# Turning the softmax probabilities with a DMA transfer instead of TensorE, in two of three attentions

## The reference, cut to what matters

```python
score = jnp.einsum('bhqd,bhkd->bhqk', q, k) / math.sqrt(DH)     # third: without bias and mask
score = score + position_bias
score = jnp.where(mask, score, -jnp.inf)
probs = jax.nn.softmax(score, axis=-1)
ctx = jnp.einsum('bhqk,bhkd->bhqd', probs, v)
out = ctx.transpose(0, 2, 1, 3).reshape(b, len_q, H * DH) @ Wo
```

## Time and profile before

| | us |
|---|---|
| median of 3 runs | 2335.64 (2335.22 to 2337.76) |
| the profiled execution's own time | 2335.8 |
| its span | 2334.0 |
| TensorE busy | 2173.6 (93%) |
| VectorE busy | 1322.0 (57%) |
| ScalarE busy | 1146.0 (49%) |
| GpSimd busy | 536.4 (23%) |
| TensorE's granted clock, mean | 0.981 of full speed |

### The profile page before, as it was taken

One profiled execution on the slowest core, in us unless ns is written; L12 is line 12 of the kernel. 1 busy time (PEld: TensorE's weight loads), 2 busy tenths in 40 slices (PEclk: granted clock), 3 DMA queues, 4 the chain that ended last, 5 costly groups with the idle time before them and its releaser, 6 DMA issues.

```text
span 2334.0 us, 40760 instructions
## 1 busy us (share of the span) xinstructions
PE 2173.6 (93%) x14284; PEld 1220.1 (52%) x14284; DVE 1322.0 (57%) x2695; ACT 1146.0 (49%) x3004; POOL 536.4 (23%) x936
## 2 busy tenths in 40 slices
PE   4799999999899899999999999998879899999998
PEld 2565555655554445555555555555434455555564
DVE  5566665666740556655656556555642455555654
ACT  4666666666412235554455544533322555666551
POOL 3332332322310312222122221212310222222221
PEclk9999999999989899999999999999979999999999
DMA  3110110110021112111111211101200111111000
GB/s 122 46 47 24 48 43 29 46 35 8 25 108 48 44 70 66 48 66 48 51 62 48 67 48 49 45 12 41 102 25 1 37 37 37 38 46 41 1 33 37
DMA packets 27366, 106.92 MB, mean 46 GB/s; under 512 B 4074, under 2 KB 12522, under 8 KB 17186
## 3 DMA queue, kind: packets, MB, share of 16 engines
q1 hardware_dynamic: 26722, 104.36, 12.7%
q10 hardware_dynamic: 448, 0.03, 0.0%
HBM read 102.29 MB, written 2.10 MB: 45 GB/s over the span
## 4 chain that ended last, share of the span: by engine, by line
PE 65%; DVE 14%; ACT 13%; issue 7%; POOL 1%; DMA 0%; ACTq 0%; DVEq 0%; POOLq 0%
PE bank L84 17%; PE bank L85 17%; PE bank L86 17%; ACT m_E L430 3%; PE bank L1788 3%; PE bank L1434 2%; PE bank L614 2%; DVE m_Sm L837 2%; ACT m_arena L311 2%; ACT m_arena L412 2%; DVE m_x L883 1%; DVE m_A L877 1%; PE bank L1334 1%; DVE m_nmax L854 1%; DVE m_arena L683 1%
## 5 line engine op out<-in xcount | busy, mean ns | idle before, releaser
L783 DVE TENSOR_TENSOR m_arena<-bank,m_arena 128x512 f16<-128x512 f32 x320 | 221.1, 691 | 507.2 <-ACT m_arena L412 505.3
L84 PE MATMUL bank<-m_input_parts,m_arena 128*128 128x512 f16 x1088 | 416.7, 383 | 8.4 <-DVE m_arena L783 2.3
L85 PE MATMUL bank<-m_input_parts,m_arena 128*128 128x512 f16 x1088 | 416.2, 383 | 0.0
L86 PE MATMUL bank<-m_input_parts,m_arena 128*128 128x512 f16 x1088 | 415.9, 382 | 0.0
L430 ACT ACTIVATE m_E<-m_Sm,m_nmax 128x64 f32<-128x64 f32 (+1 forms) x512 | 185.4, 363 | 386.5 <-DVE m_nmax L854 202.2
L895 POOL TENSOR_TENSOR m_E<-m_E,m_rinv 128x512 f32<-128x512 f32 (+1 forms) x192 | 172.5, 899 | 862.9 <-DVE m_rinv L868 862.9
L412 ACT ACTIVATE m_arena<-bank 128x512 f16<-128x512 f32 x320 | 189.7, 593 | 232.4 <-PE bank L86 231.9
L85 PE MATMUL bank<-m_wo_t,m_A 128*128 128x512 f16 x768 | 291.8, 380 | 0.0
L86 PE MATMUL bank<-m_wo_t,m_A 128*128 128x512 f16 x768 | 291.7, 380 | 0.0
L84 PE MATMUL bank<-m_wo_t,m_A 128*128 128x512 f16 x768 | 291.7, 380 | 0.0
L426 ACT ACTIVATE m_E<-bank,m_nmax,m_qk 128x128 f32<-128x128 f32 x256 | 113.8, 454 | 182.0 <-DVE m_nmax L825 182.0
(11 more groups left out here) (279 smaller groups left out, 4307.3 us busy)
## 6 DMA issues: line engine op xcount, KB each, us to landing
m_raw<-a_q SPq DMA_DIRECT2D x24, 1024.0 KB, 4.9
m_raw<-a_o SPq DMA_DIRECT2D x24, 1024.0 KB, 4.8
m_raw<-a_k SPq DMA_DIRECT2D x9, 1024.0 KB, 4.8
m_raw<-a_v SPq DMA_DIRECT2D x9, 1024.0 KB, 5.0
m_bias_in<-bias SPq DMA_DIRECT2D x64, 128.0 KB, 2.0
m_arena<-f_w SPq DMA_DIRECT2D x3, 1024.0 KB, 7.2
m_x<-x SPq DMA_DIRECT2D x2, 1024.0 KB, 7.0
m_arena<-ctx_t SPq DMA_DIRECT2D x4, 512.0 KB, 12.3
```

The lines of the kernel that those rows point to most:

```text
L84: pe.matmul(out, lhs[0], rhs[0], start=first, stop=False)
L85: pe.matmul(out, lhs[0], rhs[1], start=False, stop=False)
L86: return pe.matmul(out, lhs[1], rhs[0], start=False, stop=last)
L783: ins = dve.tensor_tensor(self.dest(name, part, 1), self.shaped(name, bank[m % 2][:, :]), self.dest(name, part, 0), ALU.subtract)
```

## The change

In the second and third attention, 60 of the 64 units (`MOVED`) are no longer transposed by TensorE. In the slot after its scores, the first thing ScalarE does for unit b-1 is to write the high part of `E` (event `split_hi`) into a new buffer `split`; VectorE writes the low part (`split_lo`) after the maxima of unit b. SP then issues one transposing transfer from `split` (128 partitions by 1024 fp16 values, high and low) to `PT`, in eight blocks of 128 x 128, with semaphores `pt0` and `pt1`. `mix` of that unit waits for the transfer, and so does `split_hi` of the unit two later. Exponentials of a unit wait for `split_lo` of the unit two earlier, where they waited for its transposes. The last four units, and the whole first attention, go the old way; the semaphores `turned_hi` and `turned_lo` are renamed to `split_hi` and `split_lo`. In SP's program the transfer of unit b-1 stands after the bias and the slab of the slot, and so ahead of those of the next slot.

```diff
@@ events
+            if self.by_dma(t, b - 1):
+                out.append(("split_hi", b - 1))
             if ok(b) and normed != 2:
                 out.append(("scores", b))
+            if self.by_dma(t, b - 1):
+                out.append(("split_lo", b - 1))
...
-            if ok(b - 1):
+            if ok(b - 1) and not self.by_dma(t, b - 1):
                 out.append(("turn", b - 1))
...
+    def by_dma(self, t, b):
+
+        return self.moved and (not isinstance(t, int) or 0 <= 8 * t + b < self.MOVED)
@@ sp
+        def turn(t, b):
+            n = 2 * HG * self.keys
+            sp.wait_ge(*s["split_lo"].by(at(t, 8, b + 1)))
+            sp.nop(nofuse=True)
+            sp.wait_ge(*s["mixed"].by(at(t, 8, b - 1)))
+            sp.nop(nofuse=True)
+            sp.dma_start_transpose(k.PT[:, b % 2].rearrange("p i n -> p (i n)")[:, 0:n].rearrange("p (h n) -> p h n", n=P),
+                                   k.split[:, b % 2].rearrange("p i n -> p (i n)")[:, 0:n])\
+                .then_inc((s["pt0"], s["pt1"])[b % 2].sem, 16)
...
+                if self.by_dma(t, slot - 5):
+                    turn(t, slot - 5)
                 if isinstance(t, int) and t == 8 and slot == 1:
                     self.next.load_tail(sp)
@@ act
                     act.wait_ge(*s["top"].by(at(t, 8, b + 1)))
-                    act.wait_ge(*s["turned"].by(at(t, 8, b - 1)))
+                    if self.moved:
+                        act.wait_ge(*s["split_lo"].by(at(t, 8, b - 1)))
+                    else:
+                        act.wait_ge(*s["turned"].by(at(t, 8, b - 1)))
...
+                elif e[0] == "split_hi":
+                    b = e[1]
+                    act.wait_ge(*s["probs"].by(at(t, 8, b + 1)))
+                    act.wait_ge(*self.pt_here(t, b - 2))
+                    act.activation(self.split_dst(b, 0), k.E[:, b % 2, 0:self.keys * HG], ACT.Copy)\
+                        .then_inc(s["split_hi"].sem, 1)
@@ pe
                     pe.wait_ge(*s["mixed_lo"].by(at(t, 8, b)))
-                    pe.wait_ge(*s["turned_lo"].by(at(t, 8, b + 1)))
+                    pe.wait_ge(*(self.pt_here(t, b) if self.by_dma(t, b) else s["split_lo"].by(at(t, 8, b + 1))))
@@ dve
+                elif e[0] == "split_lo":
+                    b = e[1]
+                    dve.wait_ge(*s["split_hi"].by(at(t, 8, b + 1)))
+                    dve.tensor_tensor(self.split_dst(b, 1), k.E[:, b % 2, 0:self.keys * HG], self.split_dst(b, 0),
+                                      ALU.subtract).then_inc(s["split_lo"].sem, 1)
```

More of the change, by code:

```diff
@@ L98 @@
     CHAIN = {"dve": {0: 0, 2: 16, 3: 8}, "pool": {0: 17, 2: 13, 3: 10}}
+    MOVED = UNITS - 4
     def __init__(self, k, layer, dram, before, before_count):
@@ L111, in __init__ @@
         self.NP, self.NK = len(self.pre), len(self.kinds)
+        self.moved = layer in (2, 3)
         names = ["raw0", "raw1", "w_ss", "w_tot", "w_scale", "w_fac", "w_hi", "w_lo", "misc", "misc_read",
                  "proj", "proj_hi", "proj_lo", "scores", "biased", "top", "exped", "rinv", "probs",
-                 "turned", "turned_hi", "turned_lo", "mixed", "mixed_hi", "mixed_lo", "outp", "xadd",
+                 "turned", "split_hi", "split_lo", "mixed", "mixed_hi", "mixed_lo", "outp", "xadd",
                  "stat", "rstd", "xn", "xt", "xt_hi", "xt_lo", "dve", "pool"]
+        names += ["pt0", "pt1"] if self.moved else []
         names += {0: ["k_tot", "k_rs", "k_n", "k_nhi", "k_nlo", "q_tot", "q_rs"],
@@ L126, in __init__ @@
         totals |= dict.fromkeys(("xn", "xt", "xt_hi", "xt_lo"), TILES)
-        totals |= dict.fromkeys(("scores", "top", "exped", "rinv", "probs", "turned", "turned_hi", "turned_lo",
+        totals |= dict.fromkeys(("scores", "top", "exped", "rinv", "probs", "split_hi", "split_lo",
                                  "mixed", "mixed_hi", "mixed_lo", "outp", "xadd"), UNITS)
+        totals |= {"turned": UNITS - self.MOVED if self.moved else UNITS}
+        totals |= {"pt0": 16 * ((self.MOVED + 1) // 2), "pt1": 16 * (self.MOVED // 2)} if self.moved else {}
         totals |= {"biased": 0 if layer == 3 else UNITS}
@@ L435, in emit @@
                     b = e[1]
-                    act.wait_ge(*s["turned"].by(at(t, 8, b + 1)))
+                    act.wait_ge(*self.turned(t, b))
                     act.wait_ge(*s["mixed"].by(at(t, 8, b - 1)))
-                    act.activation(self.pt_dst(b, 0), bank[4][:, 0:self.keys * HG], ACT.Copy).then_inc(s["turned_hi"].sem, 1)
+                    act.activation(self.pt_dst(b, 0), bank[4][:, 0:self.keys * HG], ACT.Copy).then_inc(s["split_hi"].sem, 1)
+                elif e[0] == "split_hi":
[4 more added lines that the diff above has]
+                        .then_inc(s["split_hi"].sem, 1)
                 elif e[0] == "mix":
@@ L465, in pt_dst, with split_dst, pt_here, turned @@
     def pt_dst(self, b, part):
-        return self.k.PT[:, b % 2, part, 0:self.keys * HG]
+        n = self.keys * HG
+        return self.k.PT[:, b % 2].rearrange("p i n -> p (i n)")[:, part * n:part * n + n]
+    def split_dst(self, b, part):
+        n = self.keys * HG
+        return self.k.split[:, b % 2].rearrange("p i n -> p (i n)")[:, part * n:part * n + n]
+    def pt_here(self, t, b):
+        return (self.s["pt0"], self.s["pt1"])[b % 2].by(at(t, 64, 16 * (b // 2 + 1)))
+    def turned(self, t, b):
+        return self.s["turned"].by(8 * t + b - self.MOVED + 1 if self.moved else at(t, 8, b + 1))
     def mix_src(self):
@@ L610, in emit @@
                     b = e[1]
-                    pe.wait_ge(*s["turned_lo"].by(at(t, 8, b)))
+                    pe.wait_ge(*s["split_lo"].by(at(t, 8, b)))
                     pe.wait_ge(*s["probs"].by(at(t, 8, b + 1)))
@@ L623, in emit @@
                     out = bank[5]
-                    pt_ = k.PT[:, b % 2]
+                    pt_ = [self.pt_dst(b, i) for i in range(2)]
                     if self.layer == 0:
@@ L627, in emit @@
                             lhs = [k.V[:, i, hf, b2, pt * P:(pt + 1) * P] for i in range(2)]
-                            ins = mm3(pe, out[:, b2 * HG * S:(b2 + 1) * HG * S], lhs, [pt_[:, i, 0:HG * S] for i in range(2)])
+                            ins = mm3(pe, out[:, b2 * HG * S:(b2 + 1) * HG * S], lhs, pt_)
                     elif self.layer == 2:
@@ L632, in emit @@
                             ins = mm3(pe, out[:, cols], [k.V[:, i, hf, pt, cols] for i in range(2)],
-                                      [pt_[:, i, cols] for i in range(2)])
+                                      [pt_[i][:, cols] for i in range(2)])
                     else:
@@ L870, in emit @@
                     b = e[1]
-                    dve.wait_ge(*s["turned_hi"].by(at(t, 8, b + 1)))
+                    dve.wait_ge(*s["split_hi"].by(at(t, 8, b + 1)))
                     dve.tensor_tensor(self.pt_dst(b, 1), bank[4][:, 0:self.keys * HG], self.pt_dst(b, 0),
-                                      ALU.subtract).then_inc(s["turned_lo"].sem, 1)
+                                      ALU.subtract).then_inc(s["split_lo"].sem, 1)
+                elif e[0] == "split_lo":
+                    b = e[1]
+                    dve.wait_ge(*s["split_hi"].by(at(t, 8, b + 1)))
+                    dve.tensor_tensor(self.split_dst(b, 1), k.E[:, b % 2, 0:self.keys * HG], self.split_dst(b, 0),
+                                      ALU.subtract).then_inc(s["split_lo"].sem, 1)
                 elif e[0] == "mix":
@@ L1597, in __init__ @@
             [[k.arena, 12288, 16384], [k.joint_parts[:, 2 * KC * TOK:].bitcast(FP32), 0, 4096]]
-        super().__init__(k, f"f{layer}", ["iota", "hw", "ht", "ht_s", "out"], att, dram, n, regions)
+        super().__init__(k, f"f{layer}", ["hw", "ht", "ht_s"] + (["iota", "out"] if layer == 3 else []), att, dram, n, regions)
         self.layer = layer
@@ L1781, in base @@
         if t == 2:
-            pe.wait_ge(*a["turned_lo"].by(UNITS))
+            pe.wait_ge(*a["split_lo"].by(UNITS))
             pe.wait_ge(*a["mixed_lo"].by(UNITS))
@@ L2057, in __init__ @@
         self.PT, self.A = sb("PT", [P, 2, 2, 512], FP16), sb("A", [P, 2, 2, 512], FP16)
+        self.split = sb("split", [P, 2, 2, 512], FP16)
         self.bias_in = sb("bias_in", [P, 2, 256])
```

## The result

The changed kernel takes 2302.44 us (median of 4 runs, 2297.5 to 2305.18) against 2335.43 before: ratio 0.9854, 95% interval 0.9839 to 0.9868. It is 1.5% faster; 2293 was forecast, inside a range of 2283 to 2350. The profiled execution took 2304.4 with a span of 2302.3, where 2335.8 and 2334.0 stood before: 31.4 us less, and the forecast sum was 42.9.

A forecast was written before the change was run, and what follows sets the result against it. TensorE's queue was taken to bound the second and third attention. Gains of 26.4 and 19.5 less 3 for the tails made 42.9 us off 2335.8, so forecast 2293, range 2283 to 2350.

The forecast's parts named there:

- The queue term: Second attention: 60 units each lose four transposes holding TensorE's queue 0.44 us, so 26.4 us less.
- So in the second attention I cost the transfer and SP's new waits at nothing up to T = 8: Second attention: no cost if the transfer takes up to 8 us from issue to landing; bias and slabs still in time.
- The tails: Last rounds of both attentions: small loads behind unit 59's transfer, first logits and mix 1 to 2 us late; 3 charged.
- T = 4.5: The transfer's time from issue to landing, estimated as 2.0 fixed, three times a plain load's 0.7, and 0.4 for issue.
- the slot with the tightest deadline: Third attention, after a weight conversion: landing allowed 4.0 us, so a 0.5 wait once a round, 3.8 in all.
- the 8.06: Third attention: deadline 9.8 less issue at 1.74 leaves 8.06 us for landing, minus the reduction's delay behind the scores.
- The third attention: Its gain: 23.3 us if the transfer lands soon enough, 19.5 with the expected landing time.
- The squares' wait: Third attention, one slot a round: TensorE's wait at L484 for ScalarE's squares grows by 0.4 us.
- (a): Landing takes 6 to 8 us: at 7 the third attention gains nearly nothing, 2314; at 8 all is even; 10%.
- (b): Landing takes 10 us: every mix of the third attention waits, total 2383; decides from 8 us on; 19%.
- (d): Third attention: Wo's slab, issued behind the transfer, lands 1 us late each round, 7 us, total 2300; with (c) 5%.
- (c): ScalarE and VectorE become the third attention's bound, half its gain goes, total 2304; with (d) 5%.

The follow-up runs named there:

- late_o: As tail_first, but in the second attention SP issues Wo's slab only after the scores of slot 0 of its round; 2287.95 us.
- still_turns: As tail_first, but TensorE again issues four transposes per moved unit, of the identity into a bank nobody reads; 2336.2 us.
- tail_again: The same kernel as tail_first, run on the same chip as late_o; 2295.72 us.
- tail_first: Changed kernel with the last round's bias and the dense layer's small loads issued ahead of unit 59's transfer, the wide load behind it; 2290.79 us.
- twice: As tail_first, but each transfer is made twice, the second issued when the first has landed; 2335.15 us.

## Why the prediction was right, and where its sum was off

- **The queue term** (60 x 0.44 = 26.4, second attention) was right: 57 slots took 25.2 less in late_o, at 11.71 each, and still_turns takes the gain back.
- **"So in the second attention I cost the transfer and SP's new waits at nothing up to T = 8"** is the step that failed. It asked whether bias and slab would be in time for their users, and they are. It did not ask what the slab would run beside: in the kernel before, it left 21 us ahead of the loop's return, and now it ends as TensorE gets there. That cost 6.4 of 26.4 (4.9 by tail_again, without a stretch of low clock).
- **The tails, charged 3,** cost about 11: 6.4 and 4.9 by tail_first against the changed kernel. The place and the order of events were as written (issue 6.66 into the slot, loads behind it), but the wait was 3.9 and 3.4 instead of 1 to 2. I had also not priced the clock: in the second attention's tail it was low already and stayed at 0.50 over the wait and most of Wo's products.
- **T = 4.5** was an estimate from plain loads with the moving part tripled; it is 3.0, so the slot with the tightest deadline never waits, and the 3.8 us charged for it came back. That deadline was itself wrong: the shorter chain does not bring the late reduction forward to 4.1. It starts at 2033.22 in the slot from 2028.59, 4.63 behind the scores as before, so T may be 8.06 - 4.63 = 3.4 there and not 4.0 (the 1.74 behind the 8.06 adds up to 1.72, which changes nothing), and at 4.5 the slot would have waited 1.1 and not 0.5. That this did no harm, with 0.4 to spare, is luck. Plainly copied, the same 256 KB land in 2.3. The figure of 261 GB/s in the Trainium skill ("DMA: Bandwidth & Descriptors", section on latency and other measured facts) gave an estimate of 3.0, and the trace agrees; the plain copy's 2.3, with 0.7 for moving it, leaves only 1.6 and not 2.0 for the fixed part, so the agreement may be partly chance. Eight times the 1309 ns that the Trainium skill ("VectorE: DVE Perf Modes", section on the three transpose paths) gives for one block is not what one transfer of eight blocks costs, and the advice there to prefer TensorE did not hold here, where TensorE's queue is the bound.
- **The third attention** was put at 23.3 with T short; 24.5 came once its tail was mended (587.2 to 562.7). The squares' wait grew as said: the slot that has it is 7.87 with 6.50 around it, so 1.36 of wait against 1.09 before (8.03 with 6.94), 0.3 where 0.4 was given. Not foreseen: 3.1 at unit 0.
- **Rivals.** (a) and (b) needed T of 6 and more. twice made T that long (6.1), and was even with the kernel before, where (a)'s working gives about 2305: (a)'s price was too low, in part at least because (d) comes with it. In the changed kernel (d) did not appear: the squares of Wo start 4.1 to 4.3 into the slot, as before. (c) did not appear: in free slots the reduction comes 0.87 after the scores, the floor it had before.

Sum with measured terms: 25.2 for the 57 slots without the loss at the returns (692.9 to 667.7) - 6.1 for that loss (673.8 to 667.7) - 7.4 in the last round - 1.3 in the dense layer between + 24.5 for the third attention - 4.9 for its tail + 1.7 ahead of the 57 slots (907.07 to 905.35) = 31.7, which is the difference of the two spans. The 1.3 and most of the 1.7 are scatter: the dense layer's row is 50.0 to 53.5 over the ten profiled executions, and 1.4 of the 1.7 lie ahead of the first scores. The medians differ by 33.0.

## What to carry to other kernels

Where TensorE's queue is the bound, the worth of taking instructions off it can be read from the distance between starts, and it comes in full in steady slots. What the new DMA cost here was mostly not its own latency but what it moved in the issuing queue: list each transfer behind it, with its old and new time, and look at what runs at the new time (a loop's return, a first use without a full period of cover, the last round). Issue loads that the next stage needs ahead of a transfer that waits for late data; here that reordering and one later slab gave 14.5 us more, and late_o is the best kernel of this study at 2287.95.

## What the runs showed of the hardware

- A transposing transfer of 256 KB within SBUF lands in 3.0 us, with an issue of 1.23 on SP; a plain one lands in 2.3, with 0.47.
- A 1 MB load that ended as TensorE returned to the top of its loop cost it 1.8 to 2.8 us at the return; issued after the return, 0.1. TensorE's first instruction there follows a packet of q8 by 2.6 to 2.9 us, and the load makes that packet late.
- In the last round of the second attention the clock fell to 0.50 after TensorE had been idle for 3.00 us, and stayed there over a further wait of 3.92 (changed kernel, 0.50 from 1590 to 1600); without that second wait it was back within the round (tail_first, 0.99 from 1590 to 1600). At 0.50 Wo's products start 0.43 us apart instead of 0.22.
